# Filler matmuls in TensorE's gaps of a one-core decoder block

## The reference, cut to what matters

```python
x = _layernorm(x + _L0_attn_ref(x, Wq, Wk, Wv, Wo, Wbeta, ln_w, ln_b, Wg1, Wg2, norm_w))
x = _layernorm(x + _L0_xattn_ref(x, ctx_1024, XWq, XWk, XWv, XWo, gq, gk))
x = _layernorm(x + _L0_ffn_ref(x, w_gate_up, w_down))
...
q = rmsnorm((x @ XWq).reshape(B, Sq, 16, 128), gq)
k = rmsnorm((ctx @ XWk).reshape(B, Skv, 16, 128), gk)
attn = softmax(einsum('bqhd,bkhd->bhqk', q, k) * scale)
out = einsum('bhqk,bkhd->bqhd', attn, v).reshape(B, Sq, 2048) @ XWo
...
gate, up = split(_ste(x) @ _ste(w_gate_up).T)
hq = _ste(silu(gate) * up)
out = hq @ _ste(w_down).T
```

## Time and profile before

| | |
|---|---|
| median of 3 runs | 401.19 us (397.48, 401.40, 401.19) |
| profiled execution | 397.24 us |
| its span, first to last instruction | 395.7 us |
| mean granted PE clock | 0.948 of full speed |
| busy, of the span | PE 85%, DVE 66%, ACT 48%, POOL 27% |
| instructions | 11528 |

### The profile page before, as it was taken

How to read it: one execution, slowest core, us unless ns; L and a number is a source line. 1 busy time by engine, 2 the same in 40 slices (tenths; PEclk the granted TensorE clock), 3 DMA queues, 4 the chain that set the end, 5 groups by cost and what they waited for, 6 DMA issues and landing times.

```text
span 395.7 us, 11528 instructions
## 1 busy us (share of the span) xinstructions
PE 337.1 (85%) x5050; PEld 238.5 (60%) x5050; DVE 261.3 (66%) x519; ACT 190.7 (48%) x356; POOL 107.4 (27%) x117
## 2 busy tenths in 40 slices
PE   3899978977878758499999999999999999987842
PEld 3343764434444432388697796987968879674611
DVE  0597947289799998765363764946749557394564
ACT  3043894544445335245516555565555655654210
POOL 3015395900000000000062431624415335053001
PEclk9999998999989979699999999999999999998965
DMA  8994000000410300239020200202002000000000
GB/s 251 252 321 150 1 2 6 3 5 3 131 37 3 112 2 2 65 69 204 5 56 0 55 2 15 55 0 63 8 16 53 2 15 0 15 2 13 2 1 27
DMA packets 17633, 19.99 MB, mean 51 GB/s; under 512 B 3360, under 2 KB 15024, under 8 KB 17328
## 3 DMA queue, kind: packets, MB, share of 16 engines
q1 hardware_dynamic: 17552, 19.24, 18.1%
q10 hardware_dynamic: 32, 0.02, 0.0%
HBM read 18.07 MB, written 1.18 MB: 49 GB/s over the span
## 4 chain that ended last, share of the span: by engine, by line
PE 68%; DVE 14%; ACT 7%; issue 6%; POOL 2%; DMA 1%; SPq 1%; POOLq 0%; ACTq 0%; DVEq 0%
PE ps L645 13%; PE ps L711 12%; PE ps L551 7%; PE ps L463 5%; PE ps L703 5%; PE ps L688 4%; PE ps L730 3%; PE ps L570 3%; PE ps L588 3%; PE ps L661 2%; PE ps L755 2%; PE ps L578 2%; PE ps L679 2%; PE ps L748 2%; PE ps L542 2%
## 5 line engine op out<-in xcount | busy, mean ns | idle before, releaser
L645 PEld LDWEIGHTS ps<-x1t,xwq 128*128 128x128 f32 x512 | 59.2, 192 | 7.7 <-issue 4.9
L645 PE MATMUL ps<-x1t,xwq 128*128 128x128 f32 x512 | 62.1, 278 | 1.6 <-ACT x1t L1042 1.6
L711 PE MATMUL ps<-mvo,cxp 128*128 128x256 f32 x256 | 58.2, 382 | 0.4 <-DVE gs L1464 0.4
L1592 POOL TENSOR_SCALAR rstd<-mv 128x1 f32<-128x1 f32 x22 | 4.8, 218 | 179.6 <-DVE mv L1406 179.6
L711 PEld LDWEIGHTS ps<-mvo,cxp 128*128 128x128 f32 x256 | 47.6, 190 | 6.6 <-issue 0.7
L551 PE MATMUL ps<-ctxt,xwk 128*128 128x512 f32 x64 | 37.9, 705 | 0.0
L1006 ACT ACTIVATE qt<-ps 128x512 f32<-128x512 f32 x32 | 19.1, 597 | 33.9 <-PE ps L645 33.9
L926 ACT ACTIVATE ksq<-ps 128x512 f32<-128x512 f32 x32 | 19.0, 593 | 31.7 <-PE ps L551 23.2
L928 ACT ACTIVATE kt<-ps,gks 128x512 f32<-128x512 f32 x32 | 21.9, 684 | 0.0
L588 PEld LDWEIGHTS ps<-ak,ub 32*32 32x32 f32 x1024 | 12.2, 110 | 15.8 <-issue 15.8
L1464 DVE TENSOR_TENSOR gs<-ps,s 128x352 f32<-128x352 f32 x16 | 8.4, 525 | 20.0 <-PE ps L730 20.0
(11 more groups left out here) (222 smaller groups left out, 667.0 us busy)
## 6 DMA issues: line engine op xcount, KB each, us to landing
rkb<-kscale SPq DMA_DIRECT2D x16, 256.0 KB, 4.1
xn<-in_x_dram SPq DMA_DIRECT2D x4, 512.0 KB, 5.4
ctx<-in_ctx_dram SPq DMA_DIRECT2D x4, 512.0 KB, 8.5
xwo<-in_L_xattn_Wo_dram SPq DMA_DIRECT2D x1, 2048.0 KB, 14.3
xwq<-in_L_xattn_Wq_dram SPq DMA_DIRECT2D x4, 512.0 KB, 4.4
w1n<-in_L_ffn_w_gate_up_dram SPq DMA_DIRECT2D x1, 1408.0 KB, 8.8
xwv<-in_L_xattn_Wv_dram SPq DMA_DIRECT2D x1, 1024.0 KB, 12.0
xwk<-in_L_xattn_Wk_dram SPq DMA_DIRECT2D x1, 1024.0 KB, 16.5
```

Of the source, the lines that this page charges most:

```text
L645: last = mm(bank(n % 2, P, t * P), xwq[qn][:, k * BANK + t * P:k * BANK + (t + 1) * P], x1t[:, (i % 2) * D + k * P:(i % 2) * D + (k + 1) * ...
L711: last = mm(bank(6 + turn_of[("y", i, 0)] % 2, D), cxp[:, h * P:(h + 1) * P], mvo[:, h * D:(h + 1) * D], start=h == 0, stop=h == XH - 1)
```

## The change

A function `warm(bk, n)` is added to PE's list. It issues n matmuls of the bf16 identity with the first 512 columns of `w1t`, into a PSUM bank whose content nobody reads. It waits for nothing and signals nothing. It is called in front of the main tiles (15 matmuls), and in steps 8 (12), 9 (4, 7 and 2) and 10 (16 and 4): 60 matmuls in all. Nothing else is changed.

```diff
+            def warm(bk, n):
+                for _ in range(n):
+                    mm(bank(bk), ident_b[:, :], w1t[:, 0:BANK], start=True, stop=True)
+
...
+            warm(4, 15)
             pe.wait_ge(sem("o_feat"), NCH)
             pe.wait_ge(sem("wo_scaled"), KT)
             pe.wait_ge(sem("key_emptied"), NKU)
...
                     q_quarter(i, 0)
                     q_quarter(i, 1)
+                if i == NT + 2:
+                    warm(0, 16)
                 if last3:
                     h_transpose(i - 3)
+                if i >= NT:
+                    warm(0, (12, 4, 4)[i - NT])
                 if cur:
                     q_quarter(i, 2)
...
                     q_quarter(i, 3)
                 if i == 1:
                     scores(i, range(0, 8))
+                if i == NT + 1:
+                    warm(0, 7)
                 if last2:
                     x_transpose_q(i - 2)
+                if i == NT + 1:
+                    warm(0, 2)
                 if prev:
                     context_sum(i - 1, 2)
                     context_sum(i - 1, 3)
```

## The result

The changed kernel took 395.19 us in the median of four runs (391.55 to 396.38), the kernel before 399.34 in the median of four (397.17 to 401.40). The ratio is 0.9897, with a 95% interval from 0.9853 to 0.9942: about 1% faster. The forecast was 397.6, with 394.0 to 401.0 around it. Medians are taken over all runs; a ratio compares only the fast runs of both kernels, leaving out those more than 1.5% above the fastest of their kernel.

What follows compares the result with a forecast made beforehand. PE bounds the kernel, on the chain of waits for 68% of the span, slowed where its clock falls. Terms -0.30, -0.56, -0.71 and -0.99 sum to -2.56 us; the middle of 398.6 and 396.7 gave 397.6, range 394.0 to 401.0.

Steps and rivals of the forecast that it cites:

- front: In front of the tiles: faster `ttt_out`, but perhaps a later clock fall; between -0.95 and +0.4 us, taken as -0.3.
- step 8: `p_transpose` and `ffn_down` at full clock save 1.6 us of PE time, but DVE's quantisation limits the gain: -0.56 us.
- step 9: `x_transpose_q` 0.11 us less and two pairs of `gate_up` 0.60 less at full clock: together -0.71 us.
- step 10: `h_transpose` 0.96 to 0.61 us and `ffn_down` 1.57 to 0.93, both on the chain: together -0.99 us.
- one filler, start to start: Time per 512-column bf16 filler matmul, taken as 0.23 us, between 0.16 from below and 0.45 from above.
- the fall under the queries: Front: clock fall moves from 160 to about 167 us, under 48 query records, costing 1.6 us; front then +0.4.
- The other half: Front, held equally likely: all goes well, and DVE and PE are 0.95 us early at 173.86 us.
- PE's queries ending later than `ogt`: Sign of being wrong, in front of the tiles: PE finishes its queries after DVE's `ogt`.
- the sum of 2.56: Whole kernel: -0.30 in front of the tiles, then -0.56, -0.71 and -0.99 in the last three steps, together -2.56 us.
- A: Rival, larger gain: other executions lose more to the clock and the filler takes that away too; 395.0 us, chance 0.20.
- B: Rival, nothing much: DVE and POOL swallow more of the tail, front lost at +0.4; 399.0 us, chance 0.13.
- C: Rival, slower: filler in the last steps does not hold the clock and delays work; 403.5 us, chance 0.12.

Runs made afterwards that it cites:

- tail_only: The changed kernel without the 15 filler matmuls in front of the tiles, those of steps 8 to 10 kept: 396.12 us, ratio 0.9931 to the kernel before.
- front_only: The changed kernel with only the 15 filler matmuls in front of the tiles, those of steps 8 to 10 removed: 399.37 us, ratio 0.9959.
- the traces with the hole filled: Traces of kernels adding to the changed kernel five filler matmuls before and five behind tile 0's transpose; that addition alone measured 395.15 us, ratio 0.9921.
- the longer series: The changed kernel measured again, 12 runs against 35 of the kernel before (median 399.27 us): 395.99 us, ratio 0.992.
- after_again: The changed kernel once more, nothing altered, against the kernel before: 395.99 us, ratio 0.992.
- double_filler: The changed kernel with 32 instead of 16 filler matmuls in step 10: 397.80 us in one execution.
- the early and the recurrence's filler: Filler added at the kernel's start (398.01 us; longer version 395.66) or in the recurrence's last chunk (395.02), each onto the changed kernel with tile 0's hole filled.
- early_through: Changed kernel with ten fillers around tile 0's transpose, plus nine before the first transposes and eleven before the key projection: 395.66 us, ratio 0.9874.
- early_start: Changed kernel with ten fillers around tile 0's transpose, plus nine before the first transposes and four behind them: 398.01 us, ratio 0.9958.

## Why the prediction was right

**Step by step.** From the marks above:

| term | predicted, us | measured, us |
|---|---|---|
| front | -0.95 to +0.4 | -0.94 (two traces), +0.24 to +0.25 (three traces) |
| step 8 | -0.56 | 16.50 - 17.18 = -0.68 |
| step 9 | -0.71 | 14.49 - 15.19 = -0.70 |
| step 10 | -0.99 | 5.90 - 6.87 = -0.97 |
| last three steps | -2.26 | -2.35 |
| one filler, start to start | 0.23 | 0.216 |

The limit of step 8 was read rightly: PE won 1.5 us in `p_transpose` and `ffn_down`, DVE let 0.68 of it through, and behind that PE waits for `yd` in front of `context_sum`'s second product. The profile shows 0.22 us of this wait as idle, less than the rest, since the ends of matmuls are modelled. The 0.68 is 0.12 more than forecast: `yd` starts 0.21 us behind the start of L1435 (361.54, 361.75) and not behind its end, as the prediction took it. `tail_only` and `front_only` part the terms: 36.88 and 39.10 us for the tail. The filler's 0.23 was partly luck: no row had it, it was a choice between 0.16 and 0.45, and the nearest row, scaled, gave 0.34.

**The front.** That the hole behind `ttt_out` would bring the fall under the queries was forecast as one half of the front, and the traces with the hole filled bear it out: the stretch takes 10.96 to 10.98 us in all six. The other half occurred too. The fall's price was right: the queries took 7.25 - 5.62 = 1.63 us longer, where 1.6 was forecast. Three traces lie at the one end and two at the other; their mean is -0.23, which fits the -0.3 and proves no share. The prediction contradicts itself at one place: it lists PE's queries ending later than `ogt` among the signs of being wrong. That came, at 175.08 against 174.03, and it is the +0.4 half that the prediction itself had forecast.

**The size.** Here the forecast was off. The whole came to -4.15 us between medians of four runs, and to -3.2 [-1.9, -4.5] in the longer series; the sum of 2.56 lies in the second. The number 397.6 lies 2.41 above the measured 395.19. Of this 0.86 is its base (I took 400.2 for the kernel before, whose four runs had 399.34), and the rest is the gain, 4.15 instead of 2.56. The tail's 2.35 and the front's at most 0.94 do not reach 4.15; as far as the longer series tells, part of it was the luck of four runs. Against the longer series (399.27 and 395.99) most of the error is the base, and what is left, between 2.56 and 3.2, is within the interval.

**Rivals.** A, that other executions lose more to the clock than the profiled one, is right in what it says of the spread: the first projection alone varies by 3 us, and the falls in the recurrence lie elsewhere in each trace. The mean granted clock of each run says the same: the profiled execution of before had 0.948, and 32 of the 35 runs of the longer series lie below, down to 0.915; `after_again` has 0.965 to 0.980, the profiled one after 0.969. That the filler takes such losses away too is not shown: their places are outside the filler's. A's number, 395.0, is nearer to the measured 395.19 than the forecast is, and the interval of the longer series leaves room for some of A. B's front did come, in three of five traces, but B fell by the table: the tail came in full. C fell twice: clock 1.00 through the tail in every trace with the filler there, and 0.216 us apiece, below the 0.26 from which it would decide. Its 0.28 for a stream of 352 columns at half clock does not follow from 0.78 and 0.47, which differ by 0.31; no run tests it, since the tail's filler ran at 1.00. `double_filler` shows the mechanism that C feared, by count instead of by clock.

**Open.** How often the front's hole costs its 0.25 us; whether anything beyond the tail and the front is gained, since 3.2 [1.9, 4.5] holds both 2.56 and more; whether the early and the recurrence's filler are worth anything, which six runs with a spread of 6 us cannot say; what ends the "issue" waits.

## What to carry to other kernels

Where PE stands behind another engine and the granted clock falls there, look for room for filler that waits for nothing and is through just before that engine is. Here it bought back the time of the products behind it (2.35 us in the tail), and no more than the next engine on the chain let through (0.68 of 1.5 us in step 8). Count it: start-to-start time by number against the wait, because filler beyond the wait delays the work behind it (sixteen too many cost 2.29 us). And look at what the faster clock makes of the next stretch: work that is done sooner leaves a new hole, and a fall moved from an idle place to under busy products can cost more than the one removed.

## What the runs showed of the hardware

The granted clock that a trace shows before its first change can be wrong. In the trace after, the first 16 records of the key projection take 8.69 us and the next 16, of the same shape, 7.03:

```profile
11.88 8.69 PE L463 MATMUL ps<-xt,wk 128*128 128x512 f32 x16 [1.68 <-DVE xt L1172]
...
20.41 7.03 PE L463 MATMUL ps<-xt,wq 128*128 128x512 f32 x16
```

yet the clock is shown at 1.00 in the middle of the longer ones, with 6 records in 3.2 us:

```profile
12.60:15.80 3.20, 3.20 (x6) 1.32 (x5) 0.34 (x1) 0.00 (x0) 0.29 (x1) 1.00 0.91 245
```

In `early_through` the same window has 9 records, at the same 1.00:

```profile
12.60:15.80 3.20, 3.20 (x9) 1.50 (x8) 1.17 (x2) 0.00 (x0) 0.29 (x1) 1.00 0.94 263
```

By the count of records, the longer ones ran at the lower clock: in `early_start`, where the fall is recorded, the same window has 6 records too, at 0.50.

And the same code in front of the tiles came out with a fall under the queries in one trace and without it in another (12.17 and 10.98 us), so one profile of before does not show where falls will lie in the next execution.
